# Spreading small gathers and scatters over a graph kernel's beats, and taking VectorE's low halves ahead of prelu and residual

## The reference

```python
def _sage_conv(h, src, dst, Wl, bl, Wr):
    msg = h[src]
    s = segment_sum(msg, dst, num_segments=N_NODES)
    cnt = segment_sum(ones((E, 1)), dst, num_segments=N_NODES)
    agg = s / maximum(cnt, 1.0)
    return agg @ Wl.T + bl + h @ Wr.T

h, residual = x, 0.0
for Wl, bl, Wr, g, b in params:            # three layers
    h = residual + _sage_conv(h, src, dst, Wl, bl, Wr)
    h = _layer_norm(h, g, b)
    h = where(h >= 0, h, a_prelu * h)
    residual = h
out = _layernorm(x + h)
```

## Time and profile before

| what | us |
|---|---|
| median of 3 runs | 2143.94 |
| lowest and highest | 2139.96, 2144.84 |
| the profiled execution's own time | 2149.07 |
| its span, first to last instruction | 2147.3 |
| mean granted TensorE clock | 0.987 of full speed |

### The profile page before, as it was taken

The page is one execution under the profiler, slowest core; times in us unless marked ns, Lnnn a source line. Parts: engine busy times, 40 slices in busy tenths (PEclk is TensorE's granted clock), DMA queues, the critical chain, the costliest instruction groups (busy, mean ns, idle before and its releaser), DMA issues.

```text
span 2147.3 us, 30989 instructions
## 1 busy us (share of the span) xinstructions
PE 2046.7 (95%) x10302; PEld 1683.9 (78%) x10302; DVE 1692.0 (79%) x2605; ACT 1226.3 (57%) x2565; POOL 1506.6 (70%) x1196
## 2 busy tenths in 40 slices
PE   6998999999999999999999999999999999999993
PEld 4877777788888788888888888887778888878872
DVE  6869887878887688877777777789878888888883
ACT  4864544544444355444444444478877777777775
POOL 2887877788878555655555555478887788777775
PEclk8999999999999999999999999999999999999997
DMA  5656766666666545444444444456666555565551
GB/s 181 209 201 229 220 199 199 194 205 202 210 210 210 160 153 172 160 147 148 148 147 148 148 148 148 142 192 205 213 203 191 187 189 198 184 201 187 192 171 67
DMA packets 180942, 387.46 MB, mean 180 GB/s; under 512 B 20107, under 2 KB 20552, under 8 KB 180782
## 3 DMA queue, kind: packets, MB, share of 16 engines
q1 hardware_dynamic: 142222, 271.80, 38.8%
q0 software_dynamic: 38560, 113.67, 16.1%
HBM read 220.81 MB, written 164.79 MB: 180 GB/s over the span
## 4 chain that ended last, share of the span: by engine, by line
PE 46%; POOL 22%; DVE 12%; issue 12%; ACT 7%; POOLq 0%; DMA 0%; ACTq 0%; DVEq 0%; SPq 0%
PE ps_z L408 38%; POOL y L689 8%; PE ps_t L389 5%; DVE hout L826 4%; DVE y L813 4%; POOL rstd L681 3%; PE ps_s L401 3%; POOL hin L652 2%; POOL orstd L695 2%; POOL out L706 2%; ACT junk L524 2%; ACT stage L573 2%; ACT o_sb L587 2%; DVE o_sb L868 1%; POOL node_found L730 1%
## 5 line engine op out<-in xcount | busy, mean ns | idle before, releaser
L408 PE MATMUL ps_z<-w_hi,hT_hi 128*128 128x512 f32 x1884 | 760.6, 404 | 4.2 <-DVE y L813 4.2
L408 PE MATMUL ps_z<-w_hi,hT_lo 128*128 128x512 f32 x1884 | 746.4, 396 | 0.0
L408 PE MATMUL ps_z<-w_lo,hT_hi 128*128 128x512 f32 x1884 | 745.2, 396 | 0.0
L689 POOL TENSOR_TENSOR y<-y,shift 128x1024 f32<-128x1024 f32 x235 | 605.9, 2578 | 164.8 <-DVE y L813 155.7
L524 ACT ACTIVATE junk<-ps_z 128x512 f32<-128x512 f32 x471 | 279.4, 594 | 490.3 <-DVE ps_z L805 448.1
L795 DVE TENSOR_TENSOR hT_lo<-ps_t,hT_hi 128x1024 fp32r<-128x1024 f32 (+1 forms) x237 | 287.9, 1215 | 178.3 <-ACT hT_hi L512 165.4
L408 PEld LDWEIGHTS ps_z<-w_hi,hT_lo 128*128 128x128 f32 x1884 | 355.0, 188 | 86.0
L408 PEld LDWEIGHTS ps_z<-w_hi,hT_hi 128*128 128x128 f32 x1884 | 356.3, 189 | 78.9 <-DVE y L813 2.9
L408 PEld LDWEIGHTS ps_z<-w_lo,hT_hi 128*128 128x128 f32 x1884 | 355.8, 189 | 78.5
L681 POOL TENSOR_TENSOR rstd<-veps,minus_half 128x2 f32<-128x2 f32 (+1 forms) x237 | 229.5, 969 | 259.1 <-ACT veps L530 258.6
L826 DVE SCALAR_TENSOR_TENSOR hout<-hout,slope_less,y 128x1024 f32<-128x1024 f32 (+1 forms) x237 | 377.6, 1593 | 4.0 <-ACT hout L539 4.0
(11 more groups left out here) (134 smaller groups left out, 2219.4 us busy)
## 6 DMA issues: line engine op xcount, KB each, us to landing
h_scratch<-hout SPq DMA_DIRECT2D x156, 512.0 KB
hin<-h_scratch SPq DMA_DIRECT2D x156, 512.0 KB
x_by_slot<-hin SPq DMA_DIRECT2D x78, 512.0 KB
o_sb<-x_by_slot SPq DMA_DIRECT2D x78, 512.0 KB
rowtab<-edge_row_table SPq DMA_DIRECT2D x60, 256.0 KB
stage<-in_WrT SPq DMA_DIRECT2D x3, 1024.0 KB
stage<-in_WlT SPq DMA_DIRECT2D x3, 1024.0 KB
hin<-in_x,node_get POOLq DMA_INDIRECT x157
```

The lines of the kernel that those rows point to most:

```text
L408: mm = pe.matmul(acc, a[:, k, :], ww[:, k, :], start=start, stop=stop and k == KC - 1 and a is a_lo)
L689: nc.gpsimd.tensor_tensor(y[u.r2][:, 0:u.n, :], y[u.r2][:, 0:u.n, :], moved, ALU.add).then_inc(shifted, 1)
```

## The change

`NODE_BEAT`: the 40 node gathers were at beats 4 to 15 (one each), then at the second beat of each edge unit and the beat behind it, one each, up to beat 75. Now they are at beats 2 to 19 (one each), then two each at the beat behind an edge unit (23, 27, up to 63). `PUT_BEAT`: the 40 scatters were two each at the beat behind an edge unit from 27 to 95, and four at beat 98, the last of layer 1. Now ten are at the second beat of the edge units from 26 to 62, one each; then three for each edge unit (66, 67, 67 up to 94, 95, 95), and six at beats 99 to 104, one each, in the lead of layer 2. On VectorE `take_low(ahead)` moves from behind `prelu`, `out_sum`, `take_sum_low` and the first `carry` to directly behind `add_bias(last, 1)`. Nothing is added or removed: every instruction and DMA is issued as often as before.

```diff
--- before.py
+++ after.py
@@ -221,16 +221,20 @@
         BATCH = 8
         BATCHES = -(-ET // BATCH)
         KNOWN_BEAT = [EDGE_AT[BATCH // 2 * b] - 4 for b in range(BATCHES)]
-        NODE_BEAT = [4 + t if t < BATCH + 4 else EDGE_AT[(t - BATCH - 4) // 2] + 1 + t % 2 for t in range(ET)]
-        PUT_BEAT = [EDGE_AT[t // 2 + 1] + 2 if t < ET - 2 else LAYER - 1 for t in range(ET)]
+
+        EARLY, HALF = 18, 11
+        NODE_BEAT = [2 + t if t < EARLY else EDGE_AT[(t - EARLY) // 2] + 2 for t in range(ET)]
+        PLACES = [beat + 1 for beat in EDGE_AT[1:HALF]]
+        PLACES += [beat + i for beat in EDGE_AT[HALF:len(edge_units) - 1] for i in (1, 2, 2)] + list(range(LAYER, LAYER + 8))
+        PUT_BEAT = PLACES[:ET]
         COUNT_BEAT = 0
         COUNTS_A_BEAT = 3
         TABLE_BEAT = COUNT_BEAT + 1 + -(-ET // COUNTS_A_BEAT)
         SRC_AHEAD = 6
 
         LATE = UNITS - 2
-        assert all(NODE_BEAT[t] < KNOWN_BEAT[t // BATCH] - 1 for t in range(ET)) and TABLE_BEAT + 3 < LEAD - 1 and PUT_BEAT[0] > TABLE_BEAT + 4
-        assert PUT_BEAT[-1] + 2 < EDGE_AT[len(edge_units)] - SRC_AHEAD
+        assert all(NODE_BEAT[t] < KNOWN_BEAT[t // BATCH] < PUT_BEAT[t] for t in range(ET)) and TABLE_BEAT + 3 < LEAD - 1 and PUT_BEAT[0] > TABLE_BEAT + 4
+        assert len(PUT_BEAT) == ET and PUT_BEAT[-1] + 2 < EDGE_AT[len(edge_units)] - SRC_AHEAD
 
 
         ident_in_sem, const_in_sem = sem("ident_in_sem"), sem("const_in_sem")
@@ -950,6 +954,8 @@
                 last, ahead, u, ended = done(T - 1), due(T + 1), due(T), done(T)
                 if last.exists:
                     add_bias(last, 1)
+                if ahead.exists:
+                    take_low(ahead)
                 old = done(T - 3)
                 if old.exists:
                     prelu(old)
@@ -959,7 +965,6 @@
                     take_sum_low(u, 1)
                 if ahead.exists:
                     carry(ahead, 0)
-                    take_low(ahead)
                 if last.exists:
                     normal(last)
                     add_late_shift(last)
```

## The result

The changed kernel takes 2201.56 us (median of 4, 2200.78 to 2202.14) against 2144.39 (median of 4): ratio 1.0269, 95% interval 1.0252 to 1.0287, 57 us slower. That is the direction of the forecast, at the upper edge of its range (2154 to 2202), and half as much again as the 38 us forecast.

What follows compares the result with a forecast made beforehand. The prediction took TensorE, busy 95%, as the bound, so only its waits could be won. Terms 8.5 + 16 + 19 - 5 = +38.5 us gave 2187.6 profiled, 2182 as a median, range 2154 to 2202.

Steps and rivals of the forecast that it cites:

- the circle through `out_mean`: Lead of layer 3: low half, prelu, residual adds, ScalarE's out_mean to next cast close in one beat, 8.38 us; +16 us.
- The edge part of layer 2: Edge units of layer 2: cost 0, hidden by the edge unit's two beats of matmuls with few VectorE instructions.
- The edge groups of layer 3: 16 groups of layer 3: one stall goes, but normal and GpSimd's shift come later; +1.2 a group, +19 us (-9 to +23).
- The lead of layer 2: Plain units before layer 2's first edge unit: beat 6.96 against 6.47 us, 20 beats, less 1.3 room; +8.5 us (8 to 17).
- Sum -5: Layer 1 and the moved DMAs together, shorter stalls and moved scatters against more gathers in the lead: -5 us.
- The -6: Layer 1: two stalls of 3.78 us shortened by 1.28 each, most of the clock loss back; -6 us (-2.5 to -7).
- The +3.4: Lead of layer 1: six more node gathers on a GpSimd that is 83% busy; +3.4 us, bounds 0 and 8.7.
- the -2.4 of the scatters: Start of layer 2: moving four scatters out of layer 1's last beat removes TensorE's 2.44 us wait for normal; -2.4 us.
- (a): Rival: layer 3's edge part gains and loses nothing, as GpSimd and ScalarE waits absorb it; +19.5, 2163 us, chance 0.20.
- (c): Rival: faster, as ScalarE is the later one at out_mean in layer 3; -9, 2135 us, chance 0.10.
- (d): Rival: no difference overall, gain and loss cancel; chance 0.05.
- (b): Rival: everything at its worse end, prelu stays stretched, layer 3 too; +55, 2199 us, chance 0.12.

Runs made afterwards that it cites:

- `low_only`: The kernel before with the move of take_low alone, gathers and scatters at their old beats: 2210.73 us, ratio 1.0293.
- `puts_only`: The kernel before with the new beats for the scatters alone, gathers at their old beats: 2142.70 us, ratio 0.9974.
- `beats_only`: The changed kernel with take_low back at its old place, only gathers and scatters at their new beats: 2143.01 us, ratio 0.9977.
- `low_first_in_gaps`: The changed kernel with the low half early only in beats ahead of which no unit was done, elsewhere at its old place: 2130.40 us, ratio 0.9926.
- `normal_ahead_of_sum`: The changed kernel with out_sum behind normal instead of ahead of it: 2389.95 us, ratio 1.1134.

## Why the prediction was right, and where it was wrong

**The mechanism of the move held.** The chain second bias, square, cast, low half leaves a hole that prelu filled; moved behind, it lengthens the beat in layers 1 and 2; in layer 3 the circle through `out_mean` closes in one beat. The sum for that one, 8.38 us, is what was measured (1500.90 to 1509.28), and over the 17 beats of that step the loss was 15.3 us against 16. The edge part of layer 2 cost 0.0, as said. The edge groups of layer 3 cost 17.3 against 19, 1.08 a group against 1.2. The stall that it named comes one product earlier than said, at the plain unit ahead of the edge unit, 1.32 a group. The experiments tie these losses to the move alone (`low_only`), and in the lead of layer 3 to `out_mean` (circle lengthened: 12.1 a beat). For the edge groups the prediction had the late shift on GpSimd as the cause; no run parts that from the circle through `out_mean`, so there the size was right and the cause stays open.

**The step that failed** is the sum for layer 1 and layer 2 up to its first edge unit, 8.5 - 5 = +3.5: measured were 6.1 - 4.1 - 0.6 + 12.8 = +14.2. It has two terms, and both were wrong.

**The lead of layer 2 was mis-sized.** "I take 1.28 - 0.08 = 1.20": prelu to `normal` is 1.38, as `normal` waits for its own engine's prelu. So the beat is 7.12, not 6.96, and each costs 0.65, not 0.49. The prediction's own rows had the price: in layer 3 `out_sum`, which waits for prelu in the same way, starts 1.39 after it, and that is what the sum there took. But only thirteen steps ran in the longer loop and cost 8.2 together, less than 20 times 0.65. The rest is at both ends, which the prediction had put at nothing. The two steps to the first edge unit cost 4.6, with `compare` held up by the late shift (2.50 instead of 0.34). That makes the 12.8. At the start of the layer the move cost another 2.0 (`low_only`), so that it costs 14.8 in layer 2 up to that unit, for the 8.5.

**Layer 1 and the start of layer 2 were wrong in sign.** "Sum -5": measured +6.1 - 4.1 - 0.6 = +1.4. The -6 rested on stalls shortened by 1.28 each that leave the clock alone. The move by itself did shorten them by 1.21, but the clock fell behind both and the stage lost 5.5 (`low_only`). The new scatters by themselves, for which the sum had 0 inside the edge groups, brought the same stalls to 1.82 and 1.80 with the clock at 1.00 (`puts_only`, the stage 4.0 shorter); with gathers and scatters they were 2.73 and 2.72 (`beats_only`), with the move too they were gone. The +3.4 for the six gathers was nothing (`beats_only`, -0.3); the 6.1 of the lead came with the move's own stall of 3.09, which `low_only` has as well, there for 1.8 in all. And the -2.4 of the scatters, right by itself (`beats_only`, -3.2), met the other part's loss: with the move alone the stall at the start of layer 2 is 3.83, with both 2.50. I had summed the parts as if each met the kernel before. In `low_only` and `beats_only` against the changed kernel the two parts do nearly add up (spans +59.9 and -5.5 against +52.9). How layer 1's change divides further stays open, as it moves by several us from kernel to kernel.

**Left out of the sum** were the beats at either end of the lead of layer 3: together with the edge units 218 to 228, the stages from 197 to 228 lost 18.1, 2 more than the 16; and the end of the kernel 3.3, which was not looked into. Added up: 4.3 more in layer 2's lead, 6.4 in layer 1 and the start of layer 2, 2.1 and 3.3 here, 1.7 less in the edge groups: 14.4 of 52.9 - 38.5. The profiled executions put the loss at 52.9, the medians at 57.2: the execution profiled before was 4.7 us over its median and this one 0.4, an offset that "2187.6 profiled, 2182 as a median" had carried over unchanged. The stages of layers 2 and 3 that `beats_only` and `puts_only` leave as they were repeat to 0.2 us, so this offset probably lies in layer 1, which would then have lost more than the 2.0 of the table; with one profiled execution of each kernel that isn't shown.

**Rivals.** (a), no loss in the edge groups, fell with 1.08 a group, (c) with ScalarE's 1.44 us of waiting for the add in each beat, (d) with the result. (b) had the total nearly right (2199) for reasons that didn't happen: prelu was not stretched in the leads, and the edge groups cost 17.3, not 23.

## What to carry to other kernels

An instruction's place in an in-order queue is not judged by who waits for its result alone: follow the next one queued behind it around through the other engines, and add up the circle; if it closes within one beat, its length is the beat. A hole ahead of an instruction that waits for another engine is the cheapest place for work, so bring a result forward only in the beats in which it is ready by then. Here that rule, kept to 20 beats in a layer, gave 12 us in the edge groups of layer 3 (`low_first_in_gaps`), while the same move in all beats cost 63 (`low_only`).

## What the runs showed of the hardware

Which of two colliding instructions is held up isn't told by their recorded starts alone. In the kernel before, prelu started 0.11 us ahead of the shift and was the one held up (3.60 us, the shift 2.40); elsewhere it started 0.17 ahead and kept its 1.28, and the shift took 3.36. VectorE and GpSimd, the two places, in that order:

```profile
80.03 3.60 DVE L826 SCALAR_TENSOR_TENSOR hout<-hout,slope_less,y 128x1024 f32<-128x1024 f32 x1
...
986.67 1.28 DVE L826 SCALAR_TENSOR_TENSOR hout<-hout,slope_less,y 128x1024 f32<-128x1024 f32 x1
```

```profile
79.15 0.96 POOL L730 DMA_INDIRECT node_found<-node_of_rank,rank_row  x1 [0.30 <-issue]
80.14 2.40 POOL L689 TENSOR_TENSOR y<-y,shift 128x1024 f32<-128x1024 f32 x1
...
986.84 3.36 POOL L689 TENSOR_TENSOR y<-y,shift 128x1024 f32<-128x1024 f32 x1 [1.52 <-DVE y L813]
```

The difference is what GpSimd did when prelu started. At 80.03 it was still issuing an indirect DMA (79.15 to 80.11), with the shift right behind; at 986.67 it stood idle. In the whole trace of the kernel before there are 77 places where prelu or a residual add starts up to 0.5 us ahead of a shift that it meets. In 35 of them GpSimd was at an indirect DMA at that moment, and VectorE was held up in all 35, among them 18 in which it was 0.36 to 0.41 ahead; in 42 GpSimd was idle, and the shift was the longer one in 41. The Trainium skill (SBUF — State Buffer, the part on the two sides) says that the first to start keeps the ports for its whole instruction. The places with an idle GpSimd agree; in the others VectorE's instruction did not keep them though it was recorded first, so the instruction that GpSimd is at has to be counted too. Why it matters isn't shown. In `normal_ahead_of_sum` the second add (1497.55) meets the shift (1497.70) in this way, behind a put, and it decided 2.4 us a beat.

A wait for a semaphore that the engine's own last instruction sets cost 0.18 to 0.20 us (1.38 against 1.19 us to the next start, 7.12 against 6.92 a beat).

The length of a stall of TensorE didn't tell by itself whether the granted clock fell behind it: in the kernel before the transposes behind a stall of 2.94 us took 1.07, in `low_first_in_gaps` those behind one of 2.55 took 1.94:

```profile
178.31 1.07 PE L389 MATMUL ps_t<-ident,hin 128*128 128x128 f32 x8 [2.94 <-DVE hT_lo L795]
```

```profile
295.03 1.94 PE L393 MATMUL ps_t<-ident,hin 128*128 128x128 f32 x8 [2.55 <-DVE hT_lo L799]
```
